# An attention and gated-cell kernel on one core: TensorE makes both halves of a chunk's scores in one step, and both halves of its weighing in the step behind

## The chip, the core and the metric

The kernel runs on one NeuronCore of a Trainium2 chip. The metric is device time in microseconds (us) for the whole program; lower is better. The kernel before took 745.36 us, the median of three runs (743.22 to 746.38).

The engines run side by side, each through its own list of instructions in program order: TensorE (PE, matmuls; its weight loads appear as PEld), VectorE (DVE), ScalarE (ACT), GpSimd (POOL) and SyncE (SP, which issues the DMAs). They meet only at semaphores. An instruction whose semaphore has not been reached holds up everything behind it on its own engine.

## The reference

The input x is (2, 2048, 256). The attention is one causal pass over each sequence of 2048 tokens, with 16 heads of 64, of which the values are 16 wide. Cut to what matters here:

```python
Q, K = x @ Wq.T, x @ Wk.T              # 16 heads x 64
V    = x @ Wv.T                        # 16 heads x 16
dl   = x @ Wdl.T                       # 16 heads x 12 levels
g    = -exp(A_log) * softplus(x @ Wdt.T + dt_bias)
Lam  = softplus(Lp * dl)
cg   = cumsum(g, axis=1)
W[t, s] = (Q[t] . K[s]) / 8 * exp(cg[t] - cg[s]) * Lam[t, level(t, s)]   # s <= t
Y = W @ V;  o = layernorm(Y @ Wout.T + x) * ln_g + ln_b
x1 = layernorm(x + o)
# then a two-step gated recurrence over the two sequences (sigmoid, sigmoid, tanh gates),
# h = tanh(x1 @ wo.T + c @ uo.T + bo), and out = layernorm(x1 + h)
```

level(t, s) is the bit length of t xor s. All matrices are float32; the large products are made from a high and a low part, in three matmuls each.

## The kernel before, in words

The 4096 tokens are cut into 32 chunks of 128 (`NC`); 16 chunks make a sequence. Keys of the same chunk are handled directly, keys of earlier chunks through a state S that holds one summary for each level. Two chunks form a group of 256 tokens for the projections of Q and K.

Work is put in order by a list of steps, four to a chunk (`STEPS`, s = 4 * chunk + n), and every engine walks through the same steps with its own list. For chunk ci the work that bears on the change is:

- `exponents(ci)`, PE, n = 0: 16 small matmuls (32 of the array's rows each) that write the exponents of the whole chunk into the four banks XP. It waits for the transposed levels CT (`d_ct`, DVE line 1124) and for all four weight products of the chunk before (`d_w`).
- ACT turns the four banks into E (`exps`, 4 instructions, `a_e`).
- `scores(ci, 0)`, PE, n = 1, and `scores(ci, 1)`, PE, n = 2: 8 float32 matmuls each, of 64 rows by 128 columns, which overwrite two of the XP banks with the scores of 8 heads. Each is recorded as 16 matmuls.
- `weights(ci, u)`, DVE, n = 1 and n = 2: two products of 128x512 that make W from the scores and E. It waits for `p_sc` (the scores of that half) and for `p_y`, the weighing that read this part of W before.
- `weigh(ci, 0)` and `weigh(ci, 1)`, PE, steps 4 and 5 after the chunk's first, thus in n = 0 and n = 1 of the next chunk: 8 matmuls each that multiply W with V, 32 columns of the array each, into YB. The first also waits for `d_oo`, DVE's addition of the output projection of the chunk before.
- `inter(ci)`, PE, n = 1, behind the scores: the queries against the state, 16 to 64 matmuls by the number of levels (the set bits of the chunk's number within its sequence). DVE takes it up in `inter` (tiles zt, zs), behind `weights(ci, 0)`, and that frees the two MB banks.
- `state(ci)`, PE, n = 2, behind the scores: 16 matmuls that make the new part of the state. DVE adds it to S behind `weights(ci, 1)`, and adds up levels where chunk numbers call for it.
- `out_proj(ci - 1)`, PE, n = 3, after DVE's `turn_y` (tile yt).
- One `project` of 12 matmuls in each step up to s = 118, into bank 0, which ACT copies out. Chunks 30 and 31 and the last step of chunk 29 have none.
- In n = 1 of each odd chunk up to 27: `turn_coefs` (two transposes of cf into an MB bank, free once DVE has done the first product of `inter`), then, behind the projection, `tokens` (12 matmuls of 464 columns for the group after). DVE adds the bias (tile pre), starts the softplus, and only then comes to `turn_y`, `weights(ci, 1)`, the levels C and CT, the state, and oo.
- In n = 2 of each even chunk: `decays`.

From s = 127 on the second part runs, a gated cell and the output, in blocks of 512 tokens of each sequence; it begins on PE with `first_bias`, which waits for the weight products of chunk 31 and for POOL's split of the last weights (wL).

The functions at issue are `scores` (line 392), `weigh` (402), `inter` (436), `state` (470), and the PE loop over the steps (653 to 692); on DVE `weights` (929), `inter` (939), `turn_y` (971), `state` (982), `turn_levels` (1110). Matmuls and DVE products are recorded under the lines of the helpers, 365 and 899.

Of the kernel before, what the change touches and what calls it, by code (L numbers as in the profile page):

```python
# [55 lines left out]
def project_jobs(s):  # L56
    sg, j = (s + 9) // 8, (s + 9) % 8
    return [(sg, j)] if 1 <= sg < NSG else []


def chunk_at(s, d):

    return (s - d) // 4 if s >= d and (s - d) % 4 == 0 and (s - d) // 4 < NC else None
# [34 lines left out]
STATE = {ci: n for n, ci in enumerate([c for c in range(NC) if c % CB < CB - 1])}  # L98
# [43 lines left out]
def program(nc, x, xT, wqk, wtok, wout, wffn, cst, bcv, fv, out):  # L142
    ctx = ExitStack()
    with ctx:  # L144
        scr = nc.dram_tensor("scr", (8, 8, 2, 128), F32, kind="Internal").ap()

        def sb(name, shape, dt=F32):
            return ctx.enter_context(nc.sbuf_tensor(name, shape, dt))
# [71 lines left out]
        c1 = [sb(f"c1{i}", [P, 2, 512]) for i in range(2)]  # L220
# [142 lines left out]
        def _(e):  # L363
            def mm(o, a, b, start=True, stop=True):
                return e.matmul(o, a, b, start=start, stop=stop)  # L365
# [10 lines left out]
            def exponents(ci):  # L376


                b = ci % 2
                e.wait_ge(d_ct, ci + 1)  # L380
                e.wait_ge(g_at, ci + 1)
                if ci:
                    e.wait_ge(d_w, 4 * ci)
                for j in range(4):
                    for q in range(4):
                        r = slice(32 * q, 32 * q + 32)
                        m = e.matmul(XP[q][:, :].rearrange("p (h t) -> p h t", h=H)[:, :, 8 * j:8 * j + 8], AT[b][r, j, :],  # L387
                                     CT[b][r, :].rearrange("p (h t) -> p h t", h=H)[:, :, 8 * j:8 * j + 8],
                                     start=True, stop=True, tile_position=(32 * q, 0))
                m.then_inc(p_x, 1)  # L390

            def scores(ci, u):

                c, b = ci % 2, (ci // 2) % 2
                e.wait_ge(a_e, 4 * ci + 2 * u + 2)
                for n in range(8):
                    r, j, q = 64 * (n % 2), n // 2, 4 * u + n // 2
                    m = mm(XP[2 * u + n % 2][:, 128 * j:128 * j + 128], KT[b][r:r + 64, q, 128 * c:128 * c + 128],
                           QT[b][r:r + 64, q, 128 * c:128 * c + 128])
                m.then_inc(p_sc, 1)  # L400

            def weigh(ci, u):
                sg, c = ci // 2, ci % 2
                e.wait_ge(d_w, 4 * ci + 2 * u + 2)
                if u == 0:
                    m, n = MISC["tok", sg, c]
                    e.wait_ge(m_free[m], n + 1)
                    if ci:
                        e.wait_ge(d_oo, ci)
                    if ci == 0:  # L410
                        e.wait_ge(g_v0, 3)

                for k in range(2):
                    for n in range(4):
                        h = 8 * k + 4 * u + n
                        v = 192 * k + 48 * n + 16 * u
                        y = e.matmul(YB[32 * n:32 * n + 32, 128 * k:128 * k + 128], V[sg % 3][:, c, v:v + 32],  # L419
                                     W[:, h, :], start=u == 0 and k == 0, stop=u == 1,  # L420
                                     tile_position=(0, 32 * n), skip_group_check=True)
                y.then_inc(p_y, 1)

            def keys(ci):
                c, b = ci % 2, (ci // 2) % 2
                if c == 0:
                    e.wait_ge(a_qk, 8 * (ci // 2) + 8)
                for n in range(2):
                    m, u = MISC["keys", ci, n]
                    if u:  # L430
                        e.wait_ge(m_free[m], u)
                    for q in range(4):
                        t = tr(MB[m][:, 128 * q:128 * q + 128], KT[b][:, 4 * n + q, 128 * c:128 * c + 128])
                    t.then_inc(p_kt, 1)

            def inter(ci):


                cc, c, b = ci % CB, ci % 2, (ci // 2) % 2
                if ci - 1 in MERGE:  # L440
                    e.wait_ge(d_S, MERGE[ci - 1] + 1)
                else:
                    m, u = MISC["state", ci - 1, 0]
                    e.wait_ge(m_free[m], u + 1)
                for k in range(2):
                    m, u = MISC["inter", ci, k]
                    e.wait_ge(m_free[m], u)
                for l, i, w in runs(cc):
                    for i in range(i, i + w):
                        for o in range(2):  # L450
                            for n in range(4):
                                for k in range(2):
                                    r = slice(64 * k, 64 * k + 64)
                                    t = e.matmul(MB[MISC["inter", ci, k][0]][32 * n:32 * n + 32, 128 * i:128 * i + 128],
                                                 S[r, l, n, 16 * o:16 * o + 32], QT[b][r, 4 * o + n, 128 * c:128 * c + 128],
                                                 start=i == 0 and o == 0, stop=o == 1,
                                                 tile_position=(64 * k, 32 * n), skip_group_check=True)
                        l += 1
                t.then_inc(p_in, 1)
# [10 lines left out]
            def state(ci):  # L470

                sg, c, b = ci // 2, ci % 2, (ci // 2) % 2
                m, u = MISC["state", ci, 0]
                e.wait_ge(m_free[m], u)
                km, ku = MISC["keys", ci, 0]
                e.wait_ge(m_free[km], ku + 1)
                km, ku = MISC["keys", ci, 1]
                e.wait_ge(m_free[km], ku + 1)
                e.wait_ge(g_vw, sg + 1)
                for q in range(8):  # L480
                    for h in range(2):
                        k = 64 * h
                        t = e.matmul(MB[m][k:k + 64, 16 * q:16 * q + 16], Kt[:, 128 * q + k:128 * q + k + 64],
                                     Vw[b][:, c, 128 * h + 16 * q:128 * h + 16 * q + 16], start=True, stop=True,
                                     tile_position=(0, k))
                t.then_inc(p_st, 1)

            def out_proj(ci):
                e.wait_ge(d_yt, ci + 1)
                if ci == 0:  # L490
                    e.wait_ge(l_wo, 16)
                for k in range(2):
                    t = mm(YB[:, 256:512], yt[:, 128 * k:128 * k + 128], wo[:, k, :], k == 0, k == 1)
                t.then_inc(p_op, 1)
# [158 lines left out]
            for s in STEPS:  # L653
                ci, n = s // 4, s % 4
                if 0 <= ci < NC and n == 0:
                    exponents(ci)
                if (c1 := chunk_at(s, 4)) is not None:
                    weigh(c1, 0)
                if 0 <= ci < NC:
                    if n == 0:  # L660
                        keys(ci)
                    if n == 1:
                        scores(ci, 0)
                        if ci in INTER:
                            inter(ci)
                    if n == 2:
                        scores(ci, 1)
                        if ci in STATE:
                            state(ci)
                if (c1 := chunk_at(s, 5)) is not None:  # L670
                    weigh(c1, 1)
                if (c1 := chunk_at(s, 7)) is not None:
                    out_proj(c1)
                for sg, j in token_jobs(s):
                    if j == 3:
                        decays(sg)
                    if j == 5:
                        turn_coefs(sg)
                for sg, j in project_jobs(s):
                    project(sg, j)  # L680
                for sg, j in token_jobs(s):
                    if j == 0:
                        tokens(sg)
                if s == FIRST_FFN:
                    first_bias()
                for u in units_at(s):
                    if u[0] == "g":
                        gates(*u[1:])
                    elif u[0] == "t":
                        turn_block(*u[1:])  # L690
                    elif u[1] < 16:
                        outputs(u[1])
# [781 lines left out]
```

## Time and profile before

| | us |
|---|---|
| median of three runs | 745.36 |
| lowest, highest run | 743.22, 746.38 |
| the profiled execution | 744.35 |
| its span, first to last instruction | 742.2 |
| PE busy in the span | 688.9 |
| PE weight loads busy | 595.7 |
| DVE busy | 509.0 |
| POOL busy | 357.0 |
| ACT busy | 323.0 |

The span leaves 2.15 us of the profiled execution's time outside. A matmul's recorded end is modelled, so successive matmuls overlap in the record and the distance from one start to the next is what counts. In a timeline a merged row shows the first start and the whole stretch up to the modelled end of its last matmul.

### The profile page before, as it was taken

The numbers are of one execution on the slowest core, as the hardware profiler recorded it, in microseconds if no ns is written. First come the engines' busy times: TensorE is split into PE (matmuls) and PEld (weight loads), VectorE is DVE, ScalarE is ACT, GpSimd is POOL, SyncE is SP. The second block draws the span as 40 slices with busy tenths as digits, with TensorE's granted clock in tenths as the row PEclk, the third lists the DMA queues.
The fourth block names the chain that finished last, engine by engine and source line by source line (L and its number), as shares of the span: only waits on it lengthen the run. The fifth ranks groups of instructions, "written<-read, shape, count | busy, mean of one in ns | idle before, by whom it ended". The sixth has DMA issues, their size and how long they took to land. (4 is left out here: it accounts for less than half of the span.)

```text
span 742.2 us, 21921 instructions
## 1 busy us (share of the span) xinstructions
PE 688.9 (93%) x9112; PEld 595.7 (80%) x9112; DVE 509.0 (69%) x1096; ACT 323.0 (44%) x708; POOL 357.0 (48%) x462
## 2 busy tenths in 40 slices
PE   6889999999999999999999999999958889999983
PEld 4778888888888888888888888888846678787872
DVE  3655676878688776867678687968773254575758
ACT  5545445354544344454544445354433233434321
POOL 2645564555646554655655464654541224242415
PEclk9999999999999999999999999999997999999997
DMA  8113031222315030121403041221320000010102
GB/s 282 41 36 91 6 87 27 67 42 50 65 28 91 3 91 9 54 49 45 91 2 90 13 80 35 58 55 25 82 68 0 1 1 14 15 44 15 43 7 93
DMA packets 53586, 37.06 MB, mean 50 GB/s; under 512 B 5360, under 2 KB 52080, under 8 KB 53488
## 3 DMA queue, kind: packets, MB, share of 16 engines
q1 hardware_dynamic: 53488, 35.67, 19.1%
q8 instruction: 72, 1.18, 0.7%
q14 instruction: 26, 0.21, 0.1%
HBM read 30.41 MB, written 5.24 MB: 48 GB/s over the span
## 5 line engine op out<-in xcount | busy, mean ns | idle before, releaser
L365 PE MATMUL bank<-xH,wH 128*128 128x256 f32 x480 | 145.7, 304 | 1.4 <-ACT KT L698 1.4
L365 PE MATMUL bank<-xH,wL 128*128 128x256 f32 x480 | 135.1, 281 | 0.0
L365 PE MATMUL bank<-xL,wH 128*128 128x256 f32 x480 | 135.0, 281 | 0.0
L899 DVE TENSOR_TENSOR W<-bank,E 128x512 f32<-128x512 f32 x128 | 82.2, 684 | 54.9 <-PE bank L365 54.4
L365 PEld LDWEIGHTS bank<-xH,wH 128*128 128x128 f32 x480 | 91.0, 190 | 13.3 <-issue 12.6
L365 PEld LDWEIGHTS bank<-xL,wH 128*128 128x128 f32 x480 | 91.4, 191 | 0.0
L365 PEld LDWEIGHTS bank<-xH,wL 128*128 128x128 f32 x480 | 91.0, 189 | 0.0
L698 ACT ACTIVATE QT<-bank 128x512 f32<-128x512 f32 x64 | 38.2, 596 | 106.0 <-PE bank L365 105.9
L365 PE MATMUL bank<-QT,KT 64*128 64x128 f32 x1024 | 74.4, 285 | 0.0
L698 ACT ACTIVATE E<-bank 128x512 f32<-128x512 f32 x128 | 66.1, 605 | 16.6 <-PE bank L387 16.6
L698 ACT ACTIVATE KT<-bank 128x512 f32<-128x512 f32 x64 | 38.3, 598 | 79.4 <-PE bank L365 79.3
L365 PEld LDWEIGHTS bank<-QT,KT 64*128 64x128 f32 x1024 | 62.1, 187 | 11.4 <-issue 5.2
L899 DVE TENSOR_TENSOR g<-g 128x512 f32<-128x512 f32 x24 | 16.6, 693 | 64.6 <-ACT g L698 64.3
L1262 POOL TENSOR_TENSOR lr<-mv,cs 128x1 f32<-128x1 f32 (+1 forms) x80 | 17.6, 220 | 89.1 <-DVE mv L1052 75.6
L1262 POOL TENSOR_TENSOR rs<-lr,cs 128x1 f32<-128x1 f32 (+1 forms) x80 | 56.3, 703 | 6.3
L1262 POOL TENSOR_TENSOR t<-t 128x416 f32<-128x416 f32 x45 | 48.6, 1081 | 3.6
L1262 POOL TENSOR_TENSOR xL<-xt,xH 128x512 fp32r<-128x512 f32 x15 | 19.5, 1298 | 63.4 <-ACT xH L698 63.4
L419 PE MATMUL bank<-W,V 128*32 128x128 f32 x1024 | 42.1, 283 | 2.9 <-DVE oo L899 2.7
L1262 POOL TENSOR_TENSOR x<-oo,xs 128x256 f32<-128x256 f32 x32 | 23.5, 736 | 40.1 <-DVE oo L902 40.1
L1262 POOL TENSOR_TENSOR prod<-ll,cs 128x512 f32<-128x512 f32 x32 | 41.4, 1293 | 0.5 <-DVE ll L899 0.5
L899 DVE TENSOR_TENSOR pre<-bank,bv 128x208 f32<-128x208 f32 x32 | 12.0, 375 | 41.6 <-PE bank L365 41.6
L387 PE MATMUL bank<-CT,AT 32*128 32x128 f32 x1024 | 38.5, 288 | 2.0 <-DVE CT L1124 2.0
(150 smaller groups left out, 1700.1 us busy)
## 6 DMA issues: line engine op xcount, KB each, us to landing
cB<-scr SPq DMA_DIRECT2D x240, 64.0 KB, 2.9
xt<-in_xT SPq DMA_DIRECT2D x16, 256.0 KB, 3.2
xs<-in_x SPq DMA_DIRECT2D x16, 256.0 KB, 4.2
out<-xs SPq DMA_DIRECT2D x16, 256.0 KB, 2.1
xt<-in_wffn SPq DMA_DIRECT2D x8, 256.0 KB, 3.0
QT<-in_wqk SPq DMA_DIRECT2D x4, 256.0 KB, 6.2
KT<-in_wqk SPq DMA_DIRECT2D x4, 256.0 KB, 7.3
scr<-cT SPq DMA_DIRECT2D x16, 64.0 KB, 1.9
```

The lines of the kernel that those rows point to most:

```text
L365: return e.matmul(o, a, b, start=start, stop=stop)
L387: m = e.matmul(XP[q][:, :].rearrange("p (h t) -> p h t", h=H)[:, :, 8 * j:8 * j + 8], AT[b][r, j, :], CT[b][r, :].rearrange("p (h t) -> p ...
L419: y = e.matmul(YB[32 * n:32 * n + 32, 128 * k:128 * k + 128], V[sg % 3][:, c, v:v + 32], W[:, h, :], start=u == 0 and k == 0, stop=u == 1, ...
L698: return e.activation(o, i, f, **kw)
L899: return e.tensor_tensor(o, a, b, op)
L1262: return e.tensor_tensor(o, a, b, op)
```

## The change

On TensorE alone, `weigh(c1, 1)` moves from the step after into the step of `weigh(c1, 0)`, directly behind it; `scores(ci, 1)` moves from n = 2 into n = 1, directly behind `scores(ci, 0)` and ahead of `inter(ci)`. The waits inside the functions stay as they are, and so do the lists of the other engines.

```diff
                 if (c1 := chunk_at(s, 4)) is not None:
                     weigh(c1, 0)
+                    weigh(c1, 1)
                 if 0 <= ci < NC:
                     if n == 0:
                         keys(ci)
                     if n == 1:
                         scores(ci, 0)
+                        scores(ci, 1)
                         if ci in INTER:
                             inter(ci)
-                    if n == 2:
-                        scores(ci, 1)
-                        if ci in STATE:
-                            state(ci)
-                if (c1 := chunk_at(s, 5)) is not None:
-                    weigh(c1, 1)
+                    if n == 2 and ci in STATE:
+                        state(ci)
                 if (c1 := chunk_at(s, 7)) is not None:
                     out_proj(c1)
```

PE's order in chunk ci, before and after (projection last in each step, P):

```
before  exponents weigh0(ci-1) keys P | scores0 inter weigh1(ci-1) [coefs] P [tokens] | scores1 state [decays] P | out_proj P
after   exponents weigh0 weigh1(ci-1) keys P | scores0 scores1 inter [coefs] P [tokens] | state [decays] P | out_proj P
```

## Rows read from the trace of the kernel before

**Rows 1.** The page: busy us, share of the span and instructions.

```profile
PE 688.9 (93%) x9112; PEld 595.7 (80%) x9112; DVE 509.0 (69%) x1096; ACT 323.0 (44%) x708; POOL 357.0 (48%) x462
```

**Rows 2.** Busy time by stretch: engines' busy us (instructions), PE clock, DMA share, GB/s.

```profile
50.00:543.00 493.00, 482.42 (x7786) 424.23 (x7784) 368.23 (x825) 231.32 (x545) 266.71 (x353) 1.00 0.22 51
```

**Rows 3.** Timelines of PE and DVE, chunk 18: start, us, instructions xcount [idle <-releaser].

```profile
335.48 1.09 PE L368 MATMUL bank<-cs,KT 128*128 128x128 f32 x8
336.33 0.36 PE L365 MATMUL bank<-xH,wH 128*128 128x256 f32 x1
...
337.91 1.16 PE L365 MATMUL bank<-QT,KT 64*128 64x128 f32 x16
339.00 0.67 PE L454 MATMUL bank<-QT,S 64*32 64x128 f32 x32
339.60 0.64 PE L419 MATMUL bank<-W,V 128*32 128x128 f32 x16
340.18 0.39 PE L365 MATMUL bank<-xH,wH 128*128 128x256 f32 x1
...
345.01 0.71 DVE L1124 STREAM_TRANSPOSE CT<-C 128x512 f32<-128x512 f32 x1
...
348.87 1.17 PE L387 MATMUL bank<-CT,AT 32*128 32x128 f32 x32
```

**Rows 4.** Timeline of PE in chunk 19 and into chunk 20.

```profile
354.07 1.16 PE L454 MATMUL bank<-QT,S 64*32 64x128 f32 x64
355.16 0.64 PE L419 MATMUL bank<-W,V 128*32 128x128 f32 x16
355.96 0.38 PE L368 MATMUL bank<-cs,cf 128*64 128x128 f32 x2 [0.15 <-DVE zt L899]
...
359.91 0.37 PE L365 MATMUL bank<-wtH,xL 128*128 128x464 f32 x1
360.21 1.16 PE L365 MATMUL bank<-QT,KT 64*128 64x128 f32 x16
...
366.41 1.17 PE L387 MATMUL bank<-CT,AT 32*128 32x128 f32 x32
367.51 0.65 PE L419 MATMUL bank<-W,V 128*32 128x128 f32 x16
```

**Rows 5.** Timeline of DVE in chunk 19.

```profile
354.19 1.29 DVE L899 TENSOR_TENSOR W<-bank,E 128x512 f32<-128x512 f32 x2 [2.88 <-PE bank L365]
355.39 0.75 DVE L899 TENSOR_TENSOR zt<-bank,cB 128x256 f32<-128x256 f32 x2
...
360.32 0.37 DVE L899 TENSOR_TENSOR pre<-bank,bv 128x208 f32<-128x208 f32 x1 [0.89 <-PE bank L365]
...
364.36 0.71 DVE L1124 STREAM_TRANSPOSE CT<-C 128x512 f32<-128x512 f32 x1
...
366.20 0.42 DVE L899 TENSOR_TENSOR oo<-bank,xs 128x256 f32<-128x256 f32 x1
```

**Rows 6.** Timeline of PE at the start of chunk 8.

```profile
169.42 0.65 PE L419 MATMUL bank<-W,V 128*32 128x128 f32 x16 [1.29 <-DVE oo L899]
```

**Rows 7.** Timelines of DVE and PE from chunk 15 to chunk 16.

```profile
300.97 0.71 DVE L1124 STREAM_TRANSPOSE CT<-C 128x512 f32<-128x512 f32 x1
...
301.96 1.17 PE L387 MATMUL bank<-CT,AT 32*128 32x128 f32 x32
```

**Rows 8.** Timelines of DVE and PE in chunks 30 and 31.

```profile
535.97 1.02 DVE L899 TENSOR_TENSOR zt<-bank,cB 128x384 f32<-128x384 f32 x2 [0.41 <-PE bank L454]
...
543.28 2.09 PE L387 MATMUL bank<-CT,AT 32*128 32x128 f32 x32 [2.04 <-DVE CT L1124]
...
552.66 0.27 PE L454 MATMUL bank<-QT,S 64*32 64x128 f32 x1 [1.74 <-issue]
...
552.97 1.29 DVE L899 TENSOR_TENSOR zt<-bank,cB 128x512 f32<-128x512 f32 x2 [3.00 <-PE bank L454]
...
559.52 0.77 PE L365 MATMUL bank<-wH,c0H 128*128 128x512 f32 x1 [1.08 <-issue]
```

## The prediction, made before the changed kernel ran

> **What bounds the kernel now.** I read the busy shares first. PE is busy 93% of the span, and no other engine reaches 70% [rows 1]. The view by stretches says where: from 50 to 543 us, which is chunks 1 to 30, PE is busy 482.4 of 493 us at full clock [rows 2]. A busy figure made of modelled ends can hide waits, so I then took the timeline of PE and went by starts. In an even chunk nothing stops PE: each block starts as soon as the block before it has run out [rows 3]. In an odd chunk there are two places to look at. The transposes of cf come 0.80 us after the start of a weighing that needs 0.58, because DVE has to finish its first product on the state's result first [rows 4, 5]. And behind the tokens DVE has a long list of its own, at whose end PE waits twice: the exponents need CT, the next weighing needs oo. So the bound is PE, but DVE's in-order list stands close behind it in every odd chunk, and already ends last in some [rows 6, 7].
>
> **What the change removes on PE.** No matmul is added or dropped. What changes is how often the array goes from one shape of work to another. The full-array transposes of the keys, 8 at 0.117, are followed by a projection after 0.85 us, thus after 0.03 beyond their own time: no change of shape, no loss [rows 3]. A block of scores takes 1.09 us from its start to the next block's start; inside it 16 records in 1.16 us less one modelled 0.27 give a pitch of 0.059, so 16 more of them behind the first 16 would cost 0.95. A second scores block joined to the first therefore saves 0.14. A weighing takes 0.58 from start to next start, with a pitch of 0.025, so joined it costs 0.39 and saves 0.19 [rows 3]. Sum 0.33 us for each chunk.
>
> The trace does not show three new neighbours: state results followed by a projection, projection followed by the state block, tokens followed by it. Bounds for each: 0.03 beyond the own time of the block before (keys to projection) and 0.30 from its last start (tokens to scores, the longest such step here); I take what the nearest rows give, as after a weighing (0.60 for an inter of 32 records) and as before a scores block (0.30 from the last token matmul), which leaves the sum at 0.33. Over 31 chunks these bounds lie some 7 us below and 6 us above it. That the second weighing's wait or its start adds something is bounded by 0 and 0.19, and I take 0: its `d_w` value is the one that `exponents` has already waited for.
>
> The Trainium skill, page TensorEngine Tiling (Array Packing), section Key Properties, says that a change of tiling mode drains TensorE. The trace agrees with it by the 0.14 and 0.19 beside the 0.03. By that rule alone the kernel would get some 10 us faster, and that is the first rival below.
>
> **What it moves.** PE is in order, so what goes forward pushes the rest back. Ahead of `inter` stand 0.39 (weighing) and 0.95 (scores) more than before: its result reaches DVE 1.34 us later, counted from the chunk's exponents. DVE is in order too. It does the first two W products (1.20 us), and before the change the inter result was there when it came to it or within 0.3 us: zt starts 1.20 us behind W [rows 5]. Now it waits, and behind zt stand, on DVE, the sums of the levels, the outer statistics, yt, the other two W products (whose scores are long ready), C, CT, the state and oo.
>
> Even chunks. DVE comes to CT some 1.1 to 1.4 us later than now, where CT is now done 3.15 us ahead of the exponents that need it (345.72 against 348.87) [rows 3]; the state block, two blocks behind inter, finds its bank free. So PE sees no wait, and 14 chunks (2 to 28) give 14 x 0.33 = 4.6 us.
>
> Odd chunks. The cf transposes wait for DVE's first product: last inter start, 0.31 to DVE's start (552.66 to 552.97) [rows 8], the product (0.41, half of 0.75 with the overlap), and 0.15 back to PE [rows 4, 5]. Now DVE comes 0.43 behind the last inter start (354.96 to 355.39), so of the 1.34 some 0.12 is absorbed and the tokens end 1.2 us later. With three or four levels DVE is waiting already and all 1.34 comes through; with one, where DVE is busy with W until later, 0.74 does. Behind the tokens PE has a scores block less, -1.09 [rows 4]. If nothing else waited, the chunk would lose 1.2 - 1.09 = 0.1.
>
> Something does wait. DVE's list from the last token matmul is rigid: pre 0.41 behind it, CT done 5.16 behind it, oo done 6.71 behind it [rows 4, 5]. PE now comes to the exponents 6.50 behind the last token matmul and to the next weighing 7.60 behind it; without the scores block 5.41 and 6.51. CT is then just in time. The weighing has to wait for oo plus a lag of 0.15, 6.86, so chunk 19 loses 1.2 - (7.60 - 6.86) = 0.5.
> - Chunks 3, 5, 9, 13, 19, 21, 25: between +0.1 and +0.5, by how many levels DVE adds up; 0.4 each, 2.8 us.
> - Chunks 1 and 17, one level: 0.74 - 1.09 = -0.35 each, -0.7 us.
> - Chunks 7, 11, 23, 27, where DVE also merges levels ahead of oo, and PE already waits for it up to 1.29 us [rows 6]. There the end of the tokens is what counts: all of 1.34 is lost, 5.4 us.
> - Chunk 15 has no state block, and CT ends 0.28 ahead of the exponents [rows 7]: of its 1.34 only some 0.2 comes back, 1.1 us.
> Odd chunks together: +8.6 us.
>
> The last chunks. There are no tokens and hardly a projection, and DVE's list is what ends last: the exponents of chunk 31 wait 2.04 us for CT, and the products of inter in chunks 30 and 31 start as soon as PE has made them [rows 8]. Each delay of inter goes through. Chunk 29: +1.3 on DVE, of which +0.5 is seen at the exponents of chunk 30. Chunks 30 and 31: inter cannot start now before ACT has copied the keys and freed the banks, and part of the 1.34 goes into that wait; I estimate +1.1 and +0.9, with 0 and 1.34 each as bounds; the 1.74 us of idle inside its inter, which the profile puts down to issue, I leave as it is [rows 8]. From zt of chunk 31 the chain goes over DVE and POOL to `first_bias` at 559.52, so +2.5 us enter the second part whole. The first chunk is set by DVE (the softplus of the second group), 0.
>
> **Sum.** -4.6 + 8.6 + 2.5 = +6.5 us on the profiled execution's 744.35, thus 750.9. The median of the three runs stands 1.0 above that execution, so I predict 752 us. A measurement of this kernel can tell from no change about 0.5%, 3.7 us.
>
> **Rivals.**
> 1. Fewer drains and little else: PE is at 93% [rows 1], and DVE's waits are taken up. Then 32 x 0.33 = 10.5 us are gained, less at most 1 or 2 at cf: 734 to 737 with the 1.0 added. It would decide for itself if the pushed-back products cost PE nothing, that is if DVE's list behind the tokens were over 1.1 us shorter than I read it, or if the tokens did not move. For it: the even chunks, where I expect just this. Against it: oo ends 0.35 us later than PE would come in chunk 19, and the wait of rows 6.
> 2. The lateness is halved: inter's result comes later, but DVE makes it up, because its products run faster with less of POOL beside them, or because the token move of 1.34 is nearer to 0.8. Then odd chunks cost +3 and the end +1: 744 to 747.
> 3. The clock. In chunks 8, 12, 24 and 28, where the next weighing waits, PE would stand still for up to 2.4 us instead of 1.29. The clock is 1.00 in all of this stretch now [rows 2], but after the sparse end of chunk 30 the 32 records of the exponents take 2.09 us instead of 1.17, half clock [rows 4, 8]. Two to four such falls in the middle, 1 to 2 us each, come on top of my sum: 755 to 759.
> 4. It is not done as told: the second half of the scores waits for E. ACT makes E behind the exponents, while PE has a weighing, the keys and a whole projection ahead of the scores, so I give it no time of its own.
>
> **How the numbers follow.** Forecast (747 to 755) 0.53; rival 1 0.13; rival 2 0.20; rival 3 0.11; the rest 0.03, on either side. The range leaves most of rival 1 out at the bottom and takes rival 3 in: 742 to 758. The forecast's own range, with the bounds of the unseen neighbours, is 747 to 756. Slower by over 0.5% means above 749.1: nearly all of the forecast and rival 3, 0.63. Within 0.5%: rival 2 and the forecast's lower edge, 0.23. Faster: rival 1 and a little, 0.14.
>
> **What would show it.** Even chunks should take 0.33 us less than now from exponents to exponents; the weighing should be one merged row of 32, the scores too. In odd chunks the gap between the last inter matmul and the cf transposes should be about 0.9 us in place of a weighing, and the first token matmul 1.2 to 1.3 later after the exponents. PE should show waits for oo in all odd-to-even turns but those after chunks 1, 15 and 17, summing to 6 us or more, and DVE should show waits for PE's inter (zt, zs), about 1 us in most chunks. `first_bias` should start near 566. I am wrong if the turns show no waits for oo, if the tokens do not move within the chunk, or if an even chunk gains nothing.

## The result, and the profile after

The changed kernel took 750.83 us (median of 4 runs, 749.6 to 751.73), the kernel before 744.98 us (4 runs, 743.22 to 746.38); ratio 1.0078, 95% interval [1.0056, 1.0101]: 0.8% slower, clear of the spread. The forecast was 752 against 745.36, +6.6 us; +5.85 us was measured. The profiled execution spans 749.2 us, 7.0 more than before.

First what was meant to be gained. The timeline of TensorE in chunk 18 of the changed kernel (start, us, instructions):

```profile
338.49 1.17 PE L387 MATMUL bank<-CT,AT 32*128 32x128 f32 x32
339.59 1.08 PE L419 MATMUL bank<-W,V 128*32 128x128 f32 x32
340.60 1.09 PE L368 MATMUL bank<-cs,KT 128*128 128x128 f32 x8
...
343.03 2.06 PE L365 MATMUL bank<-QT,KT 64*128 64x128 f32 x32
345.02 0.67 PE L454 MATMUL bank<-QT,S 64*32 64x128 f32 x32
...
347.23 1.11 PE L483 MATMUL bank<-Vw,Kt 128*64 128x16 f32 x32
...
350.70 1.03 PE L365 MATMUL bank<-wo,yt 128*128 128x256 f32 x4
...
353.23 1.17 PE L387 MATMUL bank<-CT,AT 32*128 32x128 f32 x32
```

Two weighings now take 1.01 us from start to next start and two scores blocks 1.99, where [rows 3] have 0.58 and 1.09 for one. From exponents to exponents the chunk takes 14.74 us; before it took 15.07. That is the 0.33.

Now an odd chunk, 19: TensorE, then VectorE, of the changed kernel, beside [rows 4, 5].

```profile
353.23 1.17 PE L387 MATMUL bank<-CT,AT 32*128 32x128 f32 x32
...
357.78 2.06 PE L365 MATMUL bank<-QT,KT 64*128 64x128 f32 x32
359.76 1.16 PE L454 MATMUL bank<-QT,S 64*32 64x128 f32 x64
361.55 0.38 PE L368 MATMUL bank<-cs,cf 128*64 128x128 f32 x2 [0.62 <-DVE zt L897]
...
365.81 1.11 PE L483 MATMUL bank<-Vw,Kt 128*64 128x16 f32 x32
```

```profile
358.99 1.29 DVE L897 TENSOR_TENSOR W<-bank,E 128x512 f32<-128x512 f32 x2 [3.32 <-PE bank L365]
360.98 0.76 DVE L897 TENSOR_TENSOR zt<-bank,cB 128x256 f32<-128x256 f32 x2 [0.70 <-PE bank L454]
...
365.92 0.38 DVE L897 TENSOR_TENSOR pre<-bank,bv 128x208 f32<-128x208 f32 x1 [0.89 <-PE bank L365]
...
369.96 0.71 DVE L1122 STREAM_TRANSPOSE CT<-C 128x512 f32<-128x512 f32 x1
...
371.80 0.42 DVE L897 TENSOR_TENSOR oo<-bank,xs 128x256 f32<-128x256 f32 x1
```

The inter matmuls start 6.53 us behind the exponents instead of 5.20, and VectorE now waits 0.70 for them. The transposes of cf come 8.32 behind the exponents instead of 7.09, the last token matmul (365.51) 12.28 instead of 11.04. From it to the end of oo VectorE needs 6.71 us, exactly as before.

Where TensorE pays for that is in its waits from 50 to 543 us (engine, line, waited for: us in total, times, longest), the changed kernel first, then the one before:

```profile
PE bank L368 <- DVE zt L897: 9.7, 13, 0.9
PE bank L419 <- DVE oo L897: 8.3, 9, 2.4
```

```profile
PE bank L368 <- DVE zt L899: 2.9, 13, 0.3
PE bank L419 <- DVE oo L899: 2.7, 3, 1.3
```

And at the start of chunk 8, where the wait was 1.29 [rows 6], the array slows down as well. Timeline of TensorE in the changed kernel, and its busy time by stretch (PE clock third from the end):

```profile
167.49 1.17 PE L387 MATMUL bank<-CT,AT 32*128 32x128 f32 x32
171.04 1.08 PE L419 MATMUL bank<-W,V 128*32 128x128 f32 x32 [2.37 <-DVE oo L897]
172.05 1.63 PE L368 MATMUL bank<-cs,KT 128*128 128x128 f32 x8
...
176.06 2.06 PE L365 MATMUL bank<-QT,KT 64*128 64x128 f32 x32
```

```profile
50.00:543.00 493.00, 472.87 (x7652) 424.74 (x7654) 348.80 (x813) 231.50 (x544) 259.12 (x345) 0.99 0.22 49
172.50:175.80 3.30, 3.30 (x17) 3.30 (x16) 1.73 (x5) 1.19 (x2) 1.75 (x3) 0.50 0.02 6
```

The granted clock of that stretch is 0.50. Keys and projection behind the weighing take 4.01 us to the scores; in chunk 18, before and after, they take 2.43. The same happens in chunk 24, behind a wait of 2.36 us.

By the starts of the exponents the difference to the kernel before runs as follows: chunk 0 +0.6 (the profiles of the other runs below begin between 0.5 us earlier and 2.2 later), chunk 8 +0.5, chunk 16 +5.3, chunk 24 +4.7, chunk 29 +8.1, `first_bias` +9.2; and the second part gives 2.2 us back.

### The profile page after: what moved, and what is told of

Same layout as the page of the kernel before. It is cut to its first block and busy times, and to the rows that moved or that the text cites. A ratio compares the mean times of both kernels' runs of the same rounds, so it can differ in the third digit from the quotient of the medians.

```text
span 749.2 us, 21921 instructions
## 1 busy us (share of the span) xinstructions
PE 681.7 (91%) x9112; PEld 597.4 (80%) x9112; DVE 496.7 (66%) x1096; ACT 324.1 (43%) x708; POOL 356.5 (48%) x462
## 5 line engine op out<-in xcount | busy, mean ns | idle before, releaser
L365 PE MATMUL bank<-QT,KT 64*128 64x128 f32 x1024 | 65.8, 278 | 0.0
L365 PEld LDWEIGHTS bank<-QT,KT 64*128 64x128 f32 x1024 | 59.7, 188 | 4.5 <-issue 0.5
L419 PE MATMUL bank<-W,V 128*32 128x128 f32 x1024 | 35.4, 280 | 8.4 <-DVE oo L897 8.3
L1260 POOL TENSOR_TENSOR Vw<-V,dv 128x128 f32<-128x128 f32 x64 | 24.6, 416 | 33.9 <-ACT dv L696 33.9
```

The costliest lines, as they stand in the source:

```text
L1260: return e.tensor_tensor(o, a, b, op)
```

## The experiments

All ratios compare with the kernel before on the same chip, whose medians there were 744.59 to 745.37 us; differences from the changed kernel go by its 750.83 above. The first four tell apart three reasons for the loss: A, the late result of inter and VectorE's fixed list behind the tokens, which is the prediction's mechanism; B, the half-clock stretches; C, the moved weighing.

**One half of the change alone: the scores.**

```diff
 # against the changed kernel
                     weigh(c1, 0)
-                    weigh(c1, 1)
...
+                if (c1 := chunk_at(s, 5)) is not None:
+                    weigh(c1, 1)
```

> Only the scores are joined; the second weighing stays in the step after, behind inter. Theory A (late inter, rigid VectorE list behind the tokens): inter comes 0.95 us later than before instead of 1.34; even chunks gain 0.14 each; odd chunks end the tokens 0.8 to 0.95 later and get back 1.09 only where VectorE's oo is not what ends last; chunks 7, 11, 23, 27 lose 0.93 each. Sum about +2 us against before, some 4 us less than the full change: 747 (745 to 749). Rival B (the loss is mainly the two stretches at half clock in chunks 8 and 24): these stay, since TensorE still stands idle over 2 us there, so 748 to 750. Rival C (the moved weighing is what costs): no slower than before, 743 to 745.

Measured 743.96 us, ratio 0.9983 [0.9966, 1.0001]: no slower than before, 3 us less than I expected of A, and outside the range that I gave it. In its profile the parts fit A all the same: the cf transposes of chunk 19 come 0.79 us later than before, and the waits for oo are as long as in the whole change. But the weighing behind inter covers most of the wait for VectorE's product. TensorE's waits from 50 to 543 us:

```profile
PE bank L419 <- DVE oo L898: 8.4, 9, 2.4
PE bank L368 <- DVE zt L898: 1.7, 7, 0.3
```

Relative to chunk 0 it stands 0.35 us earlier than before at the exponents of chunk 29. From there to `first_bias` it takes 1.4 us less than before, and the second part 1.4 less again, neither of which I had expected. TensorE stands still 2.4 us at the start of chunks 8 and 24 here too, and in the profiled execution the clock falls neither time, so B's premise that it must did not hold. But that execution, 740.70 us, is the fastest of twelve. Four took 740.70 to 742.05 us at a mean granted clock of 0.978, the other eight 743.32 to 746.94 at 0.974 or 0.972. The profile of the changed kernel, with both falls, has 0.973; the run with the weighings alone and the one with the old order in four chunks, whose waits there are 1.3 us, have 0.978 or more in all 16 executions. So the two falls probably came in the eight; no trace of one was kept. C alone would also give this time; the next run decides that.

**The other half alone: the weighings.**

```diff
 # against the kernel before
                     weigh(c1, 0)
+                    weigh(c1, 1)
...
-                if (c1 := chunk_at(s, 5)) is not None:
-                    weigh(c1, 1)
```

> Only the weighings are joined; the second half of the scores stays behind the tokens. Theory A: everything behind the first weighing in a chunk, inter and tokens too, comes 0.39 us later, the 0.57 taken out behind inter is covered in odd chunks by the wait for VectorE's first product, so odd chunks lose 0.39 each, even ones gain 0.19: +2.8 us, and about +1 in the last chunks: 749 (747 to 750). The weighing of chunk 8 waits 1.3 us as before, at full clock. Rival B: no stretch at half clock, so 744 to 746. Rival C: the whole loss of the change, 750 to 752.

Measured 748.06 us, ratio 1.0041 [1.0027, 1.0054]: 3.2 us slower, A expected 4. Even chunks gain 0.11 to 0.17 each and odd ones lose 0.40 to 0.46 each. TensorE waits longer for zt than in the whole change, and for oo as before (50 to 543 us):

```profile
PE bank L368 <- DVE zt L898: 10.3, 13, 0.9
PE bank L419 <- DVE oo L898: 2.9, 4, 1.3
```

So joining the weighings, which takes nothing but drains away, costs more than it gives when it stands ahead of what VectorE waits for. C is half right: the moved weighing is a loss, but by A's mechanism, and it is not the whole loss.

**VectorE's second half of W ahead of the tokens.**

```diff
 # against the changed kernel, on VectorE
-                if 0 <= s < NG and s % 4 in (1, 2):
-                    weights(s // 4, s % 4 - 1)
+                if 0 <= s < NG and s % 4 == 1:
+                    weights(s // 4, 0)
...
                 if 0 <= s < NG and s % 4 == 1 and s // 4 in INTER:
                     inter(s // 4)
+                if 0 <= s < NG and s % 4 == 1:
+                    weights(s // 4, 1)
```

> The full change, and VectorE makes the second half of W in step n = 1, right behind the inter products and ahead of the tokens, instead of behind them. Theory A: VectorE's list behind the last token matmul is 1.20 us shorter (CT done 4.0 behind it, oo 5.5), so TensorE's waits for oo vanish but in chunks 8 and 24 (about 1.1 us each, full clock), and the drains are gained: about 744.5 (742 to 747), 6 us below the changed kernel; the last chunks lose about 1 us because yt and the statistics come behind W. Rival B: only the half-clock stretches vanish, 748 to 749. Rival C: no change from the changed kernel, 751.

Measured 739.97 us, ratio 0.9937 [0.9923, 0.9951], 10.9 us below the changed kernel where I expected 6, and faster than before. TensorE's work is the changed kernel's, instruction by instruction. Its waits from 50 to 530 us:

```profile
PE bank L368 <- DVE zt L897: 9.7, 13, 0.9
PE bank L368 <- DVE zs L897: 1.1, 2, 0.5
PE bank L365 <- ACT KT L696: 1.1, 2, 0.8
PE bank L365 <- DVE yt L897: 0.6, 1, 0.6
```

The waits for oo are gone, the waits for zt are what they were: two separate costs. From chunk 0 to chunk 29 this run takes 12.4 us less than the changed kernel; the 8.3 of waits for oo and the 3.1 of clock make 11.4 of them. Chunk 8 was to keep a wait of 1.1 us and has none: the two VectorE additions of levels ahead of its oo are shorter here. The timelines of VectorE and of GpSimd in this run:

```profile
166.84 1.10 DVE L897 TENSOR_TENSOR S<-S 128x192 f32<-128x192 f32 x2
```

```profile
166.81 1.25 POOL L1278 TENSOR_SCALAR t<-t 128x416 f32<-128x416 f32 x1
```

And the same two of the changed kernel:

```profile
168.12 2.31 DVE L897 TENSOR_TENSOR S<-S 128x192 f32<-128x192 f32 x2
```

```profile
168.01 3.35 POOL L1260 TENSOR_TENSOR t<-t 128x416 f32<-128x416 f32 x3
```

Beside GpSimd's operations with two tensors they take 2.31 us, beside its operation with one tensor 1.10. In the changed kernel each of the two ends 0.21 us behind the GpSimd operation that was running when it started.

**The old order in the four chunks whose tokens were to cost all of 1.34 us.**

```diff
 # against the changed kernel, OLD = (7, 11, 23, 27)
+                    if ci not in OLD:
-                    weigh(c1, 1)
+                        weigh(c1, 1)
...
+                        if ci not in OLD:
-                        scores(ci, 1)
+                            scores(ci, 1)
```

(and in n = 1 and n = 2 of these chunks the two calls where they were before)

> The full change, but in chunks 7, 11, 23 and 27 TensorE keeps the order of before (second half of the scores behind the tokens, second weighing behind inter). Theory A: in these four the later end of the tokens came in full, 1.34 us each, and it set off the two half-clock stretches (1.1 us each); both go, so 7.5 us below the changed kernel: 743.5 (742 to 746). Rival B: 2.3 us below it, 748.5. Rival C: 4 of 31 weighings are back, under 1 us below it: 750.

Measured 742.89 us, ratio 0.9974 [0.996, 0.9987]; A expected 743.5. Four chunks of 32 held 8 of the change's microseconds: 4 x 1.34, and the 3.1 of the clock behind two of them. The start of chunk 8:

```profile
167.90 1.17 PE L387 MATMUL bank<-CT,AT 32*128 32x128 f32 x32
170.36 1.08 PE L419 MATMUL bank<-W,V 128*32 128x128 f32 x32 [1.28 <-DVE oo L905]
```

It is back at the wait of [rows 6], and no stretch between 50 and 541 us is at half clock.

**Inter between the halves of the scores.**

```diff
 # against the changed kernel
                         scores(ci, 0)
-                        scores(ci, 1)
                         if ci in INTER:
                             inter(ci)
+                        scores(ci, 1)
```

> The full change, but inter stands between the two halves of the scores, so that its result reaches VectorE 0.39 us later than before instead of 1.34, and the second half of the scores covers the wait for VectorE's first product; VectorE's order is that of before. Theory A: even chunks gain 0.17, the tokens end some 0.65 later in odd chunks, where 1.09 comes back except behind oo: the chunks with merges lose 0.65 each, TensorE stands still 2.4 us in chunks 8 and 24 all the same, and the clock falls there (2.3 us). About +1 against before: 746 (744 to 748), 5 us below the full change. A rival, that only the length of VectorE's list counts and not where inter stands: as the full change, 750 to 751.

Measured 744.38 us, ratio 0.9999 [0.9981, 1.0018], 6 us below the whole change: where inter stands counts, and the rival falls. The prediction for it was 746. TensorE waits 2.4 us in chunks 8 and 24 here too. Of the two expected falls of the clock the profiled execution, at 747.11 us the slowest of ten, shows one, in chunk 24.

**Both cures.**

> Inter between the two halves of the scores, and VectorE's second half of W ahead of the tokens. Theory A: the two costs (late first product, long list behind the tokens) are separate and both go. Against the run with the second half of W early alone (740), the transposes of cf come 0.6 to 0.75 us earlier in the odd chunks and no wait takes that up; even chunks lose the 0.14 of the joined scores; the last chunks gain 1 us: about 731 (728 to 735), 14 us below before. The rival, that the wait at cf is covered by something else (ACT's copies, the banks): 738 to 741.

The edit is that of the two runs together. Measured 735.99 us, ratio 0.9886 [0.9864, 0.9908]. The second cure adds to the first: 4.0 us below the run with W early alone, though not the 9 I expected. The cf transposes come 0.5 to 0.76 us earlier in the odd chunks other than 1 and 17 (there 0.34 and 0.35), without any wait:

```profile
349.82 1.16 PE L454 MATMUL bank<-QT,S 64*32 64x128 f32 x64
350.91 1.16 PE L365 MATMUL bank<-QT,KT 64*128 64x128 f32 x16
352.00 0.41 PE L368 MATMUL bank<-cs,cf 128*64 128x128 f32 x2
```

My sum was off: the odd chunks gained 7.7 us together, where 14 times 0.6 to 0.75 would be 8.4 to 10.5; unjoined scores cost 0.2 us in each even chunk and not 0.14, the last chunks gained 0.8 of the 1 us, and the second part was 1.6 us slower (last section).

**Inter first.**

```diff
 # against the changed kernel: TensorE, then VectorE
+                        if ci in INTER:
+                            inter(ci)
                         scores(ci, 0)
                         scores(ci, 1)
-                        if ci in INTER:
-                            inter(ci)
...
-                if 0 <= s < NG and s % 4 in (1, 2):
-                    weights(s // 4, s % 4 - 1)
+                if 0 <= s < NG and s % 4 == 1:
+                    if s // 4 in INTER:
+                        inter(s // 4)
+                    weights(s // 4, 0)
+                    weights(s // 4, 1)
...
-                if 0 <= s < NG and s % 4 == 1 and s // 4 in INTER:
-                    inter(s // 4)
```

> Both weighings joined, both halves of the scores joined, inter ahead of them on TensorE, and VectorE in the order inter products, first W, second W, all ahead of the tokens. Theory A: the product that cf waits for is made under the scores, and the join of the scores (0.14 a chunk) is kept: 4 us below the run with inter between: 727 (724 to 732). A rival: VectorE comes to W later, behind the sums of the levels, and the next exponents or oo wait for it: no gain over the run with inter between, 731 to 736.

Measured 737.76 us, ratio 0.9905 [0.9882, 0.9928], no better than both cures (735.99), where inter stands between the halves; the expectation was missed by 11 us. By the profile both theories are right, in different places. At the exponents of chunk 29 it is 12.6 us ahead of the kernel before (both cures: 8.7), with the odd chunks of one or two levels at 16.5 to 17.0 us in place of 17.4 to 17.6. In the odd chunks with three or four levels VectorE comes to the token products late and the state block waits up to 0.5 us for ACT's copy behind them. And from chunk 29 to `first_bias` it takes 5.3 us more than before: TensorE waits 8.6 us there for yt, which VectorE makes behind the sums of the levels and all of W, instead of 3.4.

**Each kind of chunk in the order that was best for it.**

```diff
 # against inter first, TensorE, n = 1; VectorE's calls move likewise
+MID, LATE = (7, 11, 13, 15, 23, 27), (29, 30, 31)
...
-                        if ci in INTER:
+                        if ci in INTER and ci not in MID and ci not in LATE:
                             inter(ci)
                         scores(ci, 0)
-                        scores(ci, 1)
+                        if ci in MID or ci in LATE:
+                            inter(ci)
+                        if ci not in LATE:
+                            scores(ci, 1)
```

(in LATE the second halves of scores, weighing and W stay where they were before the change, a step later)

> The best order for each kind of chunk, by what the runs showed so far: chunks up to 28 as in the run with inter first; odd chunks with three or four levels (7, 11, 13, 15, 23, 27) with inter between the halves of the scores and W ahead of the tokens; the last three chunks (29 to 31) in the order of before on both engines. Theory A, that the loss at the end comes from VectorE's own list and the gains elsewhere are additive: 12.6 us gained up to chunk 29 by inter first, 1.5 more in the chunks with many levels, nothing lost at the end: 730.5 (728 to 733). Rival: what is gained ahead of the last chunks is given back there (the last weights' loads and splits, the instruction stream): 735 to 738.

Measured 732.3 us, ratio 0.9814 [0.9792, 0.9835], 1.9% faster than the kernel before, and within the range of A. From chunk 0 to chunk 29 it gains 13.2 us, where 14.1 were expected (chunk 15 has a wait of 0.6 for oo, which neither inter first nor both cures has there), and behind that it takes what the kernel before takes. From 50 to 530 us TensorE is busy 475.25 of 480 us:

```profile
50.00:530.00 480.00, 475.25 (x7795) 425.95 (x7793) 349.79 (x827) 234.15 (x547) 267.75 (x352) 1.00 0.23 52
```

## Why the prediction was right

- **Drains.** 0.33 us a chunk was predicted; from the first weighing to the next exponents the even chunks but 8 and 24 take 0.31 to 0.35 less than before. The unseen neighbours behaved as the nearest rows: inter to projection 0.20 from last start, projection to state 0.21, tokens to state 0.30. One reading behind the bounds was wrong: a projection starts 0.03 behind the last start of the keys, not 0.03 beyond their own time (8 x 0.117 is 0.94, and it starts after 0.85). No term of the sum rests on it.
- **Tokens.** Predicted 1.2 later in chunk 19, 1.34 with three or four levels, 0.74 with one; measured 1.24, 1.30 to 1.35 and 0.79 to 0.81.
- **VectorE's list.** The 6.71 us from the last token matmul to oo did not change, and what an odd chunk loses, from its exponents to the next weighing, came out as worked out: chunk 3 +0.50 (0.5), chunk 7 +1.36 (1.34), chunk 11 +1.29 (1.34), chunk 15 +1.28 (1.1), chunk 17 -0.29 (-0.35); the seven middling ones together 2.8 (2.8). The runs with W early and with the old order in four chunks show that it is this list, and the late end of the tokens before it, that cost the time.
- **The clock, a rival.** It came as well, beside the forecast mechanism and not in its place: keys and projection took 1.6 us more in each of chunks 8 and 24, 3.1 us together. I had given it 0.11 and left it out of the sum. The Trainium skill, page TensorE: Matmul & The Clock Gate, section HAM oscillation, tells of the clock falling at waits of some 3 to 5 us for a DMA between bursts of matmuls. The trace agrees that waits bring a fall, but those here were shorter, 2.4 us; and the profile of the run with the scores alone has the same two waits and no fall.
- **The last chunks.** The term that was mis-sized: +2.5 predicted from chunk 29 to `first_bias`, +1.1 measured. Before, the 128 records of inter in chunk 31 took 3.74 us from first to last start, 2.0 of them standing still that no wait explains [rows 8]. In the changed kernel and in six of the eight experiments they take 1.75 or 1.76; in inter first it is 3.34, in the last run 2.74. So the delays around them come to some 3.1. I had left these 2.0 us as they were, without a reason. What makes them come and go was not tried.
- **The second part.** Predicted unchanged, measured 2.2 us shorter (180.5 us from `first_bias` to the end, 182.7 before). No run ties it to the change; most of it goes with the clock (last section).

So the mechanism was right, but that +6.5 came within 1 us is partly luck: +3.1 for the clock, which the sum left out, stood against -1.4 and -2.2 elsewhere. The middle, 4.0 predicted up to chunk 29, was measured at 8.1 less 0.6 of start less 3.1 of clock, 4.4.

## What to carry to other kernels

When a block is pulled forward on the engine that bounds the kernel, do not count its own cost but ask what now comes later behind it and which in-order engine waits for that: 0.33 us of drain a chunk was bought with 1.34 us of lateness. A second engine's list between two meeting points is a length to be read from the trace; if it is within the gain of the gap that it has to fit in, move its work in the same edit. With that done, and the joins kept only where they paid, this kernel came out 1.9% faster instead of 0.8% slower.

## What the runs showed of the hardware

- TensorE's clock. A stretch at half clock about 7 us behind `first_bias` splits all ten profiles in two. With it the second part takes 182.1 to 182.7 us (before, weighings alone, inter between, both cures, by chunk), without it 180.5 to 181.3 (the changed kernel, scores alone, W early, old order in four chunks, inter first). What decides is not shown: the part begins at 559.52 us with it (before) and at 559.88 without it (old order in four chunks). So some 1.5 us of a difference between two versions can come from there.
- VectorE beside GpSimd: which of the two starts first decides. Two additions of 128x192 that each started 0.11 to 0.17 us behind a GpSimd TENSOR_TENSOR took 2.31 us together, each ending 0.21 behind it; beside a TENSOR_SCALAR they took 1.10. The like addition of chunk 19 starts 0.02 us ahead of the TENSOR_TENSOR beside it and takes 0.36, and there it is GpSimd's that is long, 1.27 us instead of 1.06.
- Behind a wait of 2.4 us in the middle of full work the clock fell to half in chunk 8 and in chunk 24 of the profiled execution of the changed kernel, in one of the two with inter between, and in neither with the scores alone, though the clocks of its other executions speak for falls in eight of twelve. Behind waits of 1.2 to 1.3 us there it fell in no profile. In a version with the longer waits some 3 us of the time may thus come and go from one execution to the next; no pair of traces of one version was kept that would show it.
